# A scan and mixture-of-experts kernel on one NeuronCore: VectorE makes the product with B one pair further ahead of the scans

## What is computed

```
xn = layernorm(x)
# branch s: a selective scan (d: 128 channels, n: 64 states)
left, right = split(layernorm(xn) * gamma + beta) @ W_up + b_up
u = silu(conv3(left));  delta = softplus(u @ W_delta + b_delta)
B = u @ W_B;  C = u @ W_C;  A = -exp(A_log)
h[t] = exp(delta[t] * A) * h[t-1] + (delta[t] * u[t]) * B[t]      # 128 x 64 states
y[t] = sum_n h[t] * C[t] + u[t] * D
s = xn + (y * silu(right)) @ W_down + b_down
# branch ffn: 8 experts, each token goes to its best two
ffn = sum over the two experts of weight * ((silu(xn @ w1) * (xn @ w3)) @ w2)
out = x + s * silu(ffn)
```

## Time and profile before

| | |
|---|---|
| median of 3 runs | 1383.98 us (1377.9 to 1392.47) |
| the profiled execution, device time | 1385.34 us |
| its span in the profile | 1382.9 us |
| busy share of the span: PE, DVE, POOL, ACT | 87%, 86%, 79%, 53% |
| from 700 to 900 us, busy: PE, DVE, POOL, ACT | 187.95, 177.08, 167.28, 111.17 of 200 us |

### The profile page before, as it was taken

The page is one execution under the profiler, slowest core; times in us unless marked ns, Lnnn a source line. Parts: engine busy times, 40 slices in busy tenths (PEclk is TensorE's granted clock), DMA queues, the critical chain, the costliest instruction groups (busy, mean ns, idle before and its releaser), DMA issues.

```text
span 1382.9 us, 26003 instructions
## 1 busy us (share of the span) xinstructions
PE 1205.3 (87%) x7688; PEld 938.9 (68%) x7688; DVE 1193.4 (86%) x1634; ACT 734.1 (53%) x1583; POOL 1089.5 (79%) x1048
## 2 busy tenths in 40 slices
PE   4846788999999999998899989998999999989761
PEld 4725366877677777876687768686777777877530
DVE  6747588999799998989798979898989988988988
ACT  1361556555655565546554565456545565545642
POOL 0346278898899788888998788788979788988994
PEclk8579999999999999999999999999999999999655
DMA  7111264646364645564556436643664457464458
GB/s 211 61 39 46 67 212 135 168 141 214 110 175 143 198 148 165 147 212 121 148 147 211 126 119 180 214 142 103 172 211 139 127 155 230 143 222 149 144 175 291
DMA packets 124316, 216.51 MB, mean 157 GB/s; under 512 B 15040, under 2 KB 40768, under 8 KB 124160
## 3 DMA queue, kind: packets, MB, share of 16 engines
q10 hardware_dynamic: 73728, 134.25, 33.9%
q1 hardware_dynamic: 43616, 61.83, 13.6%
q0 software_dynamic: 6816, 18.62, 4.2%
HBM read 190.67 MB, written 23.99 MB: 155 GB/s over the span
## 4 chain that ended last, share of the span: by engine, by line
PE 68%; POOL 9%; issue 8%; DVE 6%; DMA 4%; ACT 3%; SPq 1%; ACTq 0%; DVEq 0%; POOLq 0%
PE bank L1222 31%; PE bank L1192 14%; PE bank L1170 8%; PE bank L1236 6%; POOL arena L433 4%; DMA wring<-in_w_all 3%; PE bank L1099 2%; POOL hid L448 2%; DVE arena L964 2%; PE bank L1115 1%; PE bank L1135 1%; PE bank L1068 1%; PE bank L1061 1%; SPq L386 1%; PE bank L1205 1%
## 5 line engine op out<-in xcount | busy, mean ns | idle before, releaser
L433 POOL TENSOR_TENSOR arena<-arena,c_rep 128x512 f32<-128x512 f32 x512 | 607.1, 1190 | 153.4 <-DVE arena L964 145.6
L964 DVE TENSOR_TENSOR_SCAN arena<-bank,carry,arena 128x512 f32<-128x512 f32 x512 | 652.5, 1275 | 30.7 <-ACT bank L733 30.5
L1222 PEld LDWEIGHTS bank<-xgT,wring 128*128 128x128 f32 x4288 | 518.3, 194 | 138.4 <-issue 99.3
L1222 PE MATMUL bank<-xgT,wring 128*128 128x128 f32 x4288 | 540.6, 280 | 50.5 <-issue 26.4
L733 ACT ACTIVATE bank<-arena,a_neg 128x512 f32<-128x512 f32 x512 | 354.2, 692 | 107.7 <-ACT bank L733 43.2
L955 DVE TENSOR_TENSOR arena<-bank,b_rep 128x512 f32<-128x512 f32 x512 | 351.8, 687 | 42.6 <-PE bank L1236 23.4
L662 ACT ACTIVATE th<-bank 128x256 f32<-128x256 f32 x284 | 108.9, 383 | 347.0 <-PE bank L1222 324.9
L1236 PE MATMUL bank<-stack,pick 128*128 128x512 f32 x512 | 279.1, 546 | 8.3 <-DVE arena L955 7.9
L1192 PE MATMUL bank<-wring,hid 128*128 128x256 f32 x1072 | 271.4, 386 | 8.2 <-POOL hid L448 7.4
L1192 PEld LDWEIGHTS bank<-wring,hid 128*128 128x128 f32 x1072 | 196.1, 191 | 64.4 <-issue 24.6
L448 POOL TENSOR_TENSOR hid<-gt,ue 128x256 f32<-128x256 f32 x284 | 209.6, 738 | 15.4 <-DVE gt L976 11.8
(11 more groups left out here) (172 smaller groups left out, 818.9 us busy)
## 6 DMA issues: line engine op xcount, KB each, us to landing
arena<-delta_d ACTq DMA_DIRECT2D x512, 256.0 KB
wring<-in_w_all SPq DMA_DIRECT2D x64, 384.0 KB, 5.6
xn<-in_x SPq DMA_DIRECT2D x4, 1024.0 KB, 9.9
xn_d<-xn SPq DMA_DIRECT2D x4, 1024.0 KB, 5.5
parts_d<-spare SPq DMA_DIRECT2D x16, 256.0 KB
stack<-parts_d SPq DMA_DIRECT2D x16, 256.0 KB, 5.7
wring<-results SPq DMA_DIRECT2D x8, 512.0 KB, 7.3
arena<-results SPq DMA_DIRECT2D x8, 512.0 KB, 7.9
```

Of the source, the lines that this page charges most:

```text
L433: pool.tensor_tensor(p_ring[:, s % P_RING, :], h_ring[:, s % H_RING, :], of_chunk(c_rep, c, 2), ALU.mult).then_inc(s_hc, 1)
L964: v.tensor_tensor_scan(out=h_ring[:, s % H_RING, :], data0=a_bank[s % 2][:, :], data1=b_ring[:, s % B_RING, :], initial=carry[:, q:q + 1], ...
L1222: ins = pe.matmul(bank[:, m * SW + r * SLOT:m * SW + (r + 1) * SLOT], wring[:, 2 * j + r, (2 * m + h) * P:(2 * m + h + 1) * P], xgT[:, i % ...
```

## The change

`mult` gets four tiles instead of two: `b_ring` now has the tiles 16, 17, 22 and 23 of the arena. 22 and 23 held the transposed columns `colsT` of odd chunks in the first stage, which now lie in `gt` and `ue`; the weights `w_in`, loaded to `ue` before, go to `xg`. VectorE does `mult(0)` ahead of its loop, and in turn `s` it does `mult(s + 1)` where `mult(s)` stood. `mult(s + 1)` waits for `spread(s + 1)` and, with four tiles, for `scan(s - 3)`. TensorE's code and the two PSUM banks `du_bank` are as before.

```diff
-H_RING, P_RING, B_RING, D_RING = 8, 8, 2, 4
+H_RING, P_RING, B_RING, D_RING = 8, 8, 4, 4
...
-        w_in = ue[:, :, 0:P]
+        w_in = xg[:, :, 0:P]
...
-        colsT = (xgT[:, :, :, :].rearrange("p (x a) h t -> p x (a h t)", x=2), ring[:, 22:24, :])
+        xgT_rows = xgT[:, :, :, :].rearrange("p (x a) h t -> p x (a h t)", x=2)
+        colsT = ((xgT_rows[:, 0, :], xgT_rows[:, 1, :]), tuple(a[:, :, :].rearrange("p k t -> p (k t)") for a in (gt, ue)))
...
-        b_ring = ring[:, H_RING + P_RING:H_RING + P_RING + B_RING, :]
-        dl_ring = ring[:, H_RING + P_RING + B_RING:H_RING + P_RING + B_RING + D_RING, :]
+        b_ring = [ring[:, k, :] for k in (16, 17, 22, 23)]
+        dl_ring = ring[:, 18:18 + D_RING, :]
...
-                v.tensor_tensor(b_ring[:, s % B_RING, :], du_bank[s % 2][:, :], b_rep[:, cols(c)], ALU.mult).then_inc(s_bm, 1)
+                v.tensor_tensor(b_ring[s % B_RING], du_bank[s % 2][:, :], b_rep[:, cols(c)], ALU.mult).then_inc(s_bm, 1)
...
+            mult(0)
             for s in range(PAIR_COUNT):
-                mult(s)
+                if s + 1 < PAIR_COUNT:
+                    mult(s + 1)
                 if s:
                     scan(s - 1)
                     gates(BY_PAIR[s - 1])
```

More of the change, by code:

```diff
@@ L554, in _ @@
                     for h in range(2):
-                        ins = act.activation(colsT[c % 2][:, h, :], banks[2 * (c % 2) + h][:, :], ACT.Copy)
+                        ins = act.activation(colsT[c % 2][h], banks[2 * (c % 2) + h][:, :], ACT.Copy)
                     ins.then_inc(s_xev, 1)
@@ L578, in evict_columns @@
                     src = banks[h] if c == 0 else gu_bank[h]
-                    ins = act.activation(colsT[c % 2][:, h, :], src[:, :], ACT.Identity,
+                    ins = act.activation(colsT[c % 2][h], src[:, :], ACT.Identity,
                                          bias=vec[:, 2 + h:3 + h], scale=vec[:, h:h + 1])
@@ L964, in scan @@
                 v.tensor_tensor_scan(out=h_ring[:, s % H_RING, :], data0=a_bank[s % 2][:, :],
-                                     data1=b_ring[:, s % B_RING, :], initial=carry[:, q:q + 1],
+                                     data1=b_ring[s % B_RING], initial=carry[:, q:q + 1],
                                      op0=ALU.mult, op1=ALU.add).then_inc(s_scan, 1)
@@ L1067, in logits @@
                     for h in range(2):
-                        ins = pe.matmul(banks[6][:, (c * TC + n) * E:(c * TC + n + 1) * E], colsT[c % 2][:, h, n * P:(n + 1) * P],
+                        ins = pe.matmul(banks[6][:, (c * TC + n) * E:(c * TC + n + 1) * E], colsT[c % 2][h][:, n * P:(n + 1) * P],
                                         gsb[:, h, :], start=(h == 0), stop=(h == 1))
@@ L1098, in left_right @@
                     for h in range(2):
-                        ins = pe.matmul(bank[:, :], wup[:, h, m * P:(m + 1) * P], colsT[c % 2][:, h, :],
+                        ins = pe.matmul(bank[:, :], wup[:, h, m * P:(m + 1) * P], colsT[c % 2][h],
                                         start=(h == 0), stop=(h == 1))
```

## The result

| | change | before, same chips |
|---|---|---|
| median | 1479.18 us (4 runs, 1476.23 to 1482.69) | 1384.56 us (4 runs, 1377.9 to 1392.47) |
| profiled execution, device time | 1482.69 us | 1385.34 us |

The ratio is 1.069 (95% interval 1.066 to 1.073), so the change costs 95 us. The forecast was 1426 us, with 1460 as the upper end. The direction was right, the size was not.

The account below looks back on a forecast made before the run. The prediction took TensorE, with 68% of the chain, as the bound. To 1385.3 us it added 29 (expert tiles), 5 (hidden values) and 14.5 (loop start), less 8 given back: 1426 us, range 1390 to 1460.

## What to carry to other kernels

An instruction moved ahead in one engine's list needs its input moved ahead in the other engine's list as well; else a busy engine gives its lead away and everything behind the waiting instruction is late. Put what is ready ahead of what must wait: the same work in the order scan, one-hot tiles, product, gates took 1377 us, and 1479 with the product first. And when a lead is lost, price every deadline of the pattern from the last real wait, with the late engine's own rate, and add the clock where TensorE is left idle.

## What the runs showed of the hardware

- In this kernel a wait of TensorE was paid a second time. After 5.26 us of idle time a batch of eight matmuls took 2.23 us instead of 1.13, and eight later ones behind 1.31 us of idle time took 5.40 instead of 3.70. 92 added transpositions, whose results nobody reads, made the kernel about 8 us faster.
- A product on VectorE that waits for the scan right ahead of it starts 0.11 us after the scan's end, and one that need not wait 0.08 before it. In every turn of the loop this made 31 us. The Trainium skill (VectorE: DVE Perf Modes, The DRAIN you can't avoid) says of a chain of eight copies that "the semaphore costs nothing extra here". It does not carry over to these instructions, as this pair of runs, 1408.39 and 1377.16 us, shows.
